# Pairing the value products of two key tiles, and multiplying query weights early, in a two-layer cross-attention kernel

## What is computed

```python
x = x + _L0_xattn_ref(_layernorm(x), ctx_2048, itok, ...)   # 16 heads, latent keys, 9 keys per query, rope
x = x + _L0_ffn_ref(_layernorm(x), ...)                     # shared expert + 8 experts, 2 chosen
x = x + _L1_xattn_ref(_layernorm(x), ctx_2048, ...)         # 16 heads of 16, all 1601 keys
x = x + _L1_ffn_ref(_layernorm(x), ...)
# in the first attention
q_c = q @ W_dq
q_nope = (q_c @ W_uq).reshape(b, lq, H, HD)
k_nope = (kv_c @ W_uk).reshape(b, lk, H, HD)
# in the second attention
attn = softmax(einsum('bnhd,bmhd->bhnm', q, k) * scale)     # over 1601 keys
o = einsum('bhnm,bmhd->bnhd', attn, v).reshape(B, N, C)
out = _qdq(o) @ _qdq(wp).T + bp
```

## Time and profile before

| | |
|---|---|
| median of 3 runs | 819.45 us (819.33 to 820.27) |
| profiled execution, its own time | 820.73 us |
| its span | 818.9 us |
| TensorE busy | 757.7 us (93%) |
| TensorE weight loads | 428.6 us (52%) |
| VectorE busy | 565.7 us (69%) |
| ScalarE busy | 383.9 us (47%) |
| GpSimd busy | 197.3 us (24%) |
| granted TensorE clock, mean | 0.979 of full speed |

### The profile page before, as it was taken

One profiled execution on the slowest core, in us unless ns is written; L12 is line 12 of the kernel. 1 busy time (PEld: TensorE's weight loads), 2 busy tenths in 40 slices (PEclk: granted clock), 3 DMA queues, 4 the chain that ended last, 5 costly groups with the idle time before them and its releaser, 6 DMA issues.

```text
span 818.9 us, 13086 instructions
## 1 busy us (share of the span) xinstructions
PE 757.7 (93%) x5026; PEld 428.6 (52%) x5027; DVE 565.7 (69%) x1290; ACT 383.9 (47%) x562; POOL 197.3 (24%) x208
## 2 busy tenths in 40 slices
PE   7999999977989989879999999999999999899996
PEld 3545767753745655644444454654455554345434
DVE  4687989531446566597787878777787777897814
ACT  2100443443423223216666657466666566574670
POOL 2298313220930131110220402300505001300000
PEclk9799999999999999999999999999999999999999
DMA  9200000205298330445055282550380820560000
GB/s 302 124 0 1 1 1 1 81 0 184 72 132 146 104 49 20 49 58 88 2 116 67 81 152 31 120 75 2 142 121 15 143 39 1 107 76 14 2 1 14
DMA packets 32476, 55.94 MB, mean 68 GB/s; under 512 B 11572, under 2 KB 20532, under 8 KB 31509
## 3 DMA queue, kind: packets, MB, share of 16 engines
q1 hardware_dynamic: 32408, 55.04, 33.5%
HBM read 42.56 MB, written 12.46 MB: 67 GB/s over the span
## 4 chain that ended last, share of the span: by engine, by line
PE 68%; DVE 18%; issue 6%; POOL 4%; ACT 2%; DMA 1%; SPq 0%; DVEq 0%; POOLq 0%; ACTq 0%
PE ps L1096 12%; PE ps L985 12%; PE ps L1075 9%; PE ps L873 5%; DVE small L1656 5%; PE ps L883 3%; PE ps L752 3%; PE ps L949 3%; PE ps L929 3%; PE ps L799 2%; PE ps L842 2%; PE ps L759 2%; PE ps L830 2%; DVE small L1606 1%; PE ps L1057 1%
## 5 line engine op out<-in xcount | busy, mean ns | idle before, releaser
L1656 DVE TENSOR_REDUCE small<-ps 128x1 f32<-128x400 f32 (+1 forms) x512 | 285.9, 572 | 83.1 <-PE ps L985 77.0
L1467 ACT ACTIVATE r<-ps 128x1024 f32<-128x1024 f32 (+1 forms) x208 | 212.6, 1024 | 90.4 <-PE ps L1075 87.7
L985 PE MATMUL ps<-r 96*128 96x400 bf16 (+1 forms) x512 | 171.3, 342 | 14.6 <-DVE small L1656 12.1
L1096 PE MATMUL ps<-r 128*17 128x256 f32 (+1 forms) x1664 | 131.2, 387 | 2.3 <-ACT r L1467 2.0
L1075 PE MATMUL ps<-r 99*128 99x256 bf16 (+1 forms) x832 | 126.5, 274 | 0.0
L985 PEld LDWEIGHTS ps<-r 96*128 96x128 bf16 x512 | 49.6, 97 | 127.3 <-DVE small L1656 93.4
L1075 PEld LDWEIGHTS ps<-r 99*128 99x128 bf16 (+1 forms) x832 | 81.6, 100 | 31.7 <-issue 9.5
L633 POOL TENSOR_TENSOR r<-r 128x400 bf16<-128x400 f32 (+1 forms) x32 | 29.4, 951 | 202.4 <-ACT r L1308 202.4
L929 PE MATMUL ps<-r,hT 128*128 128x512 f32 (+1 forms) x160 | 69.1, 564 | 0.0
L873 PE MATMUL ps<-r,wkvT 128*128 128x400 f32 (+1 forms) x128 | 53.4, 516 | 5.5 <-issue 5.5
L883 PE MATMUL ps<-wkvT,r 128*128 128x256 f32 (+1 forms) x208 | 55.5, 383 | 0.0
(11 more groups left out here) (201 smaller groups left out, 1028.4 us busy)
## 6 DMA issues: line engine op xcount, KB each, us to landing
r<-kscr SPq DMA_DIRECT2D x96, 200.1 KB, 8.8
kscr<-r SPq DMA_DIRECT2D x24, 400.2 KB, 3.8
r<-in_ctx_dram SPq DMA_DIRECT2D x4, 1601.0 KB, 7.0
r<-qscr SPq DMA_DIRECT2D x24, 128.0 KB, 5.0
r<-in_wo_dram SPq DMA_DIRECT2D x1, 2048.0 KB, 12.0
r<-in_gu_dram SPq DMA_DIRECT2D x1, 2048.0 KB, 7.7
qscr<-qpart SPq DMA_DIRECT2D x24, 64.0 KB, 1.7
x<-in_x_dram SPq DMA_DIRECT2D x1, 1024.0 KB, 5.3
```

What stands on the lines that cost most here:

```text
L985: mm(bank(ca % 2)[:, 0:m], qst[0:SROWS, h, q0:q0 + P], kst[0:SROWS, s % 2, h % HALF, a:a + m], start=True, stop=True).then_inc(mx_mm, 1)
L1096: last = mm(bank(6)[32 * k:32 * k + VW, 0:LQ], vx[0:n, b % 2, kt, h, :], pr[i % 3][0:n, k * LQ:(k + 1) * LQ], start=kt == 0, stop=kt == KT ...
L1467: fn(pr[i % 3][0:n, :], bank(2 + 2 * (i % 2), 2)[0:n, :], ACT.Exp, scale=SCALE1)\
L1656: v.tensor_reduce(mxc[quad % 2][:, n:n + 1], bank(ca % 2)[:, 0:m], AX_X, ALU.max).then_inc(mx_rdy, 1)
```

## The change

Three things. In the second layer `weigh` runs in pairs: in even steps from kt = 2 on, for the two steps before; in kt = 0 for the one before (the last of the quad before); in odd steps not at all. The chunks of maxima that `pace` puts between the two `weigh` of a pair are cut into four matmuls of 32 queries each, on the four quarters of the array's columns (`parted`). `step_work` counts the columns of the value products where they now are, so the shares of the steps in the chunks move too. In the first layer the 16 heads of L731 are issued four at a time behind the transposes of tiles 3 to 6, and the first half of L738 behind tile 5; ScalarE's copies are interleaved to match.

```diff
+def weighed(quad, kt):
+
+    i = KT * quad + kt
+    if kt == 0:
+        return [i - 1] if quad else []
+    return [i - 2, i - 1] if kt % 2 == 0 and quad < QUADS else []
+
-def step_work(jobs):
+def step_work(jobs, kt):
...
-    return 4 * LQ + 4 * LQ + sum(cost.get(kind(j), 0) for j in jobs)
+    return 4 * LQ + 4 * LQ * len(weighed(1, kt)) + sum(cost.get(kind(j), 0) for j in jobs)
@@ tensor, first layer
             for t in range(TILES):
...
                 last.then_inc(xnT_mm, 1)
-            pe.wait_ge(ld_q, 96)
-            for h in range(H):
-                last = mm(bank(h // 8)[0:QC, (h % 8) * KVC:(h % 8 + 1) * KVC], wuq[:, h, :], wuk[:, h, :],
-                          start=True, stop=True)
...
+                if t == 3:
+                    pe.wait_ge(ld_q, 96)
+                if t >= 3 and t < 7:
+                    for h in range(4 * (t - 3), 4 * (t - 3) + 4):
+                        last = mm(bank(h // 8)[0:QC, (h % 8) * KVC:(h % 8 + 1) * KVC], wuq[:, h, :], wuk[:, h, :],
+                                  start=True, stop=True)
+                        if h % 8 == 7:
+                            last.then_inc(m_mm, 1)
+                if t == 5:
+                    query_down(0)
+            query_down(1)
@@ max_scores
-                mm(bank(ca % 2)[:, 0:m], qst[0:SROWS, h, q0:q0 + P], kst[0:SROWS, s % 2, h % HALF, a:a + m],
-                   start=True, stop=True).then_inc(mx_mm, 1)
+                width = P // 4 if parted else P
+                for r in range(0, P, width):
+                    last = mm(bank(ca % 2)[r:r + width, 0:m], qst[0:SROWS, h, q0 + r:q0 + r + width],
+                              kst[0:SROWS, s % 2, h % HALF, a:a + m], start=True, stop=True)
+                last.then_inc(mx_mm, 1)
@@ the step
-                        if quad or kt:
-                            weigh(KT * quad + kt - 1)
-                        pace(4 * LQ)
+                        for i in weighed(quad, kt):
+                            weigh(i)
+                            pace(4 * LQ, parted=i < KT * quad + kt - 1)
@@ scalar, first layer
             for t in range(TILES):
...
                    ACT.Copy).then_inc(xnT_ev, 1)
+                if t == 5:
+                    act.wait_ge(ld_q, 96)
+                    weights_made(0)
+                elif t == 6:
+                    query_down(0)
+            weights_made(1)
+            query_down(1)
```

More of the change, by code:

```diff
@@ L100, in schedule @@
         window = range(max(0, first), first + KT)
-        work = [chunk_room(beside.get((i // KT, i % KT), [])) for i in window]
+        work = [chunk_room(beside.get((i // KT, i % KT), []), i % KT) for i in window]
         done, placed = 0, 0
@@ L119, in tail_bank, with chunk_room @@
     return 7 if b + 1 < B else {"turn_x": 5, "up": 0, "gate": 1, "down": 2, "expert": 3}.get(part, 7)
-def step_work(jobs):
+def weighed(quad, kt):
[4 more added lines that the diff above has]
+def step_work(jobs, kt):
     cost = {"k": 8 * 401, "v": 16 * D, "out": 2 * 4 * P, "shift": 8 * P, "up": 16 * D, "down": 16 * D,
             "expert": 16 * D, "turn_x": 4 * 4 * P, "turn_o": 4 * P, "project": 4 * D, "gate": 4 * 4 * E}
-    return 4 * LQ + 4 * LQ + sum(cost.get(kind(j), 0) for j in jobs)
-def chunk_room(jobs):
+    return 4 * LQ + 4 * LQ * len(weighed(1, kt)) + sum(cost.get(kind(j), 0) for j in jobs)
+def chunk_room(jobs, kt):
     busy = {"out": 2 * 2 * D, "bias": 2 * 2 * D, "scale": 3 * 2 * D, "round": 4 * 2 * D, "project": 2 * 2 * D,
@@ L133, in chunk_room @@
             "gate": 2 * 2 * D, "down": 3 * 2 * D, "expert": 2 * 2 * D}
-    return max(0, step_work(jobs) + 1969 - 0.6 * sum(busy.get(kind(j), 0) for j in jobs))
+    return max(0, step_work(jobs, kt) + 1969 - 0.6 * sum(busy.get(kind(j), 0) for j in jobs))
 def first_chunks(t, third):
@@ L718, in _, with query_down @@
             mm(bank(6), wkrs, kf0[1][0:KVC, :], start=True, stop=True).then_inc(rope_mm, 1)
+            def query_down(hf):
+                pe.wait_ge(xnT_ev, 4 * hf + 4)
+                for c in range(FC):
+                    last = mm(bank(4 - hf)[0:QC, :], wdq[:, c, :], xnT[:, c, hf * 512:(hf + 1) * 512], start=c == 0,
+                              stop=c == FC - 1)
+                last.then_inc(qc_mm, 1)
             for t in range(TILES):
@@ L971, in turn_q, with max_scores @@
                 last.then_inc(q1T_mm, 1)
-            def max_scores(quad, n):
+            def max_scores(quad, n, parted=False):
                 b, s, u, c = quad // 4, quad // 2, n // len(CH), n % len(CH)
@@ L1212, in _, with pace @@
                     others = [j for j in jobs if j[0] != "max"]
-                    total, count = step_work(others), len(maxima)
+                    total, count = step_work(others, kt), len(maxima)
                     passed = [0]
-                    def pace(columns):
+                    def pace(columns, parted=False):
                         passed[0] += columns
                         while maxima and (count - len(maxima)) * total < count * passed[0]:
-                            max_scores(*maxima.pop(0)[1:])
+                            max_scores(*maxima.pop(0)[1:], parted)
                     if quad < QUADS:
@@ L1248, in _, with weights_made, query_down @@
             fn(kvtok, bank(5)[:, 0:B * KVC].rearrange("p (b n) -> p b n", b=B), ACT.Copy).then_inc(kvt_ev, 1)
+            def weights_made(g):
+                act.wait_ge(m_mm, g + 1)
+                src = bank(g)[0:QC, :].rearrange("p (h n) -> p h n", h=8)
+                fn(weff[:, 8 * g:8 * g + 8:2, R:P], src[:, 0::2, :], ACT.Copy)
+                fn(weff[:, 8 * g + 1:8 * g + 8:2, 0:KVC], src[:, 1::2, :], ACT.Copy).then_inc(m_ev, 1)
+            def query_down(hf):
+                act.wait_ge(qc_mm, hf + 1)
+                fn(qcT[:, hf * 512:(hf + 1) * 512], bank(4 - hf)[0:QC, :], ACT.Copy).then_inc(qc_ev, 1)
             for t in range(TILES):
```

## The result

| | before | after |
|---|---|---|
| median of 9 runs | 820.27 us (818.32 to 822.75) | 824.25 us (820.99 to 828.18) |
| profiled execution, its own time | 820.73 us | 823.2 us |
| its span | 818.9 us | 821.4 us |

The account below looks back on a forecast made before the run. TensorE was taken to set the pace, VectorE at 76%. Second layer -16.9 + 6.3 + 11.0 = +0.4 and first layer -1.7 sum to -1.3, a median of 818.2 us; own range 815 to 822, 8 in 10 within 811 to 828.

Parts of the forecast that it names:

- The pairs, -16.9 us: Second layer: 89 pairs of value products (W) with a quartered chunk (m) between save 0.19 us each, -16.9 us.
- m is dear: Rival: second layer's quartered chunk (m) costs 0.1 to 0.5 us more, giving around 828, up to 850; chance 0.13.
- The chunks' waits, +6.3: Second layer: after 30 two-chunk odd steps the next step's first chunk waits 0.21 us for its bank, +6.3 us.
- `shift`, +11.0: Second layer, quad ends: `shift` waits for VectorE's `nst`, 0.49 us in eight quads, up to 1.24 elsewhere, +11.0 us.
- What is late next: shift: Step on second layer's quad ends: with one value product gone, `shift` must wait for `nst`, +11.0 us.
- Longer idling drops the clock: Rival, second layer: longer waits bring half clock in two to four more quads, +3.4 to +6.8, 822 to 825; chance 0.14.
- The first layer, -1.7: First layer: heads and L738's first half fill TensorE's idle time between transposes, costed at half clock, -1.7 us.
- rises a stretch earlier: First-layer case: the clock may rise earlier since L738's work now begins at 22.2, giving 29.8, 2.5 us earlier.
- my own sign: Second layer: the prediction is wrong if the steps' stretch is over 5 us shorter or longer.
- The waits are hidden: Rival, second layer: say half of the 17.3 us of waits does not appear, giving 809.5; chance 0.17.
- No change: Rival: neither layer changes, clock rising late and small costs cancelling, 819.5; no chance of its own, inside forecast's range.

Follow-up runs that it names:

- experiment 3: Changed kernel with the chunk between a pair's two value products left whole on 128 columns, not quartered; 844.9 us, 1.0295 to the kernel before.
- Experiment 6: Changed kernel with pairs of value products in odd steps 3 to 11 and single ones in steps 0, 1 and 12; 816.88 us, 0.9957 to the kernel before.
- experiment 2: Kernel before with only the second layer's parts of the change, first layer untouched; 827.78 us, 1.0084 to the kernel before.
- experiment 1: Kernel before with only the first layer's part of the change, second layer untouched; 816.52 us, 0.9955 to the kernel before.
- experiment 4: Changed kernel with a quad's chunks of maxima ending one step earlier, in kt = 9 instead of 10; 821.54 us, 1.0009 to the kernel before.
- 5 even shares: Kernel of experiment 4 with the constant in `chunk_room` cut from 1969 to 400; 819.57 us, 0.9994 to the kernel before.
- experiment 7: Kernel of Experiment 6 with the constant in `chunk_room` cut from 1969 to 400; 811.52 us, 0.9894 to the kernel before.

## Why the prediction was wrong

**The pairs, -16.9 us: right, and under-sized.** 0.22 us a pair in the timelines of the changed kernel and of experiment 3, against the 0.19 I counted. The sums have -22.8 us for the steps, with the pairs of quad 15, which I had at 0.06 us each and left out; they gain nothing. "m is dear" is refuted by 0.17 us from start to start; its four narrow weight loads take 0.12 us together (553.69, above), beside the W in front, and do not show in the time. The estimate by the Trainium skill (TensorE: Matmul & The Clock Gate, LDWEIGHTS) was 107 ns for the four one behind the other. The trace does not bear it out: one load of a whole chunk has a record of 0.10 us and the four narrow ones 0.12 together, so they overlap.

**The chunks' waits, +6.3: the mechanism right, the sum too high.** The 0.2 us waits are in the trace where I put them. But chunks wait only 2.0 us more in all. 2.9 us of the difference are the two waits that now stand in front of `shift` (above). The rest may be that VectorE catches up while TensorE stands before `shift`, which I named and took nothing off for; no run isolates it.

**`shift`, +11.0: +14.0**, or 11.1 without the 2.9 us that were chunk waits before. In five undisturbed quads it is 0.57 us (forecast 0.49), in quads 4 and 8 1.14 (1.24), in quads 0 and 14 0.88 and 0.86 (0.86 each), in the three late ones 2.1 to 2.2 (2.4, 1.9 and 1.9). What I did not see is quads 5, 9 and 13, 1.4 each in place of 0.62. The timeline of the first of them:

```profile
527.87 0.17 DVE L1691 TENSOR_TENSOR nst<-small,nst 128x8 bf16<-128x8 f32 x1
527.96 0.88 DVE L1845 SCALAR_TENSOR_TENSOR y<-ps,small,mag 128x256 f32<-128x256 f32 x2
...
528.89 0.61 PE L1073 MATMUL ps<-identb,nst 128*3 128x128 bf16 x8 [1.31 <-DVE y L1845]
```

`nst` is ready at 528.04, but `shift` writes bank 7, and that is free only when VectorE has made `y` from it, 0.8 us later. I had traced the data of `shift` and not its bank. In time it mattered little: behind the same operation TensorE stood 0.3, 0.3 and 1.3 us in these quads before.

**The step that failed: "What is late next: shift".** I stopped there, and the terms for K, V, the tail and the clock stood at nothing. The W's in odd steps had covered a second kind of wait, that of K, V and the tail for bank 7 and ScalarE's copies out of it; I noted for those steps only that they have matmuls enough "and do not wait". The timeline of one:

```profile
571.66 0.59 ACT L1332 ACTIVATE r<-ps,bk 128x400 bf16<-128x400 f32 x1
...
572.30 0.94 PE L886 MATMUL ps<-r,wkvT 128*128 128x400 f32 x2 [0.39 <-ACT r L1332]
```

By the sums K waits 3.8 us, V 1.9 and the tail 5.2, where before the three had 1.9 together: **+9.0 us that no term of mine held**. No experiment isolates them. Experiment 6, which moves the pairs to the odd steps but keeps bare steps, leaves them nearly as they are (4.2, 0.6, 5.0) and is faster than the changed kernel even so, which speaks for a price of pairing rather than of the place of the pairs, but does not show it. W itself waits 0.8 less.

**The clock.** I had "Longer idling drops the clock" as a rival with 0.14, at 822 to 825, and the median lies there. That is partly luck: the rival counted with the other terms as I had them, and their errors cancel (+6.9 and +1.9 against -5.9 and -2.4, below). The profile has 13.7 us at half clock in the steps for 6.8, at the late `shift`s where the forecast looked: one drop is new (584.60), one is where it was, and one is longer (704.07 to 710.90, 6.83 us). That is +3.4, the low end of the rival's price, in one more quad and not in two to four. The profile of experiment 2 has the same three. Over all executions the change is smaller: the mean granted clock falls from 0.9785 to 0.9765 by the second layer's parts alone, and from 0.983 (experiment 1) to 0.979 with them on top, worth 1.3 and 2.5 us by the slope in the last section.

That long waits bring the drop is not shown. The wait of 1.64 us was followed by one before and is followed by none in experiment 1's profile, and experiment 6 has waits of 1.97, 2.07 and 2.51 us in the same quads and full clock through all its steps. With the clock's +3.4 but without the missed +9.0, and with the pairs at their real price, the second layer would have come out slightly ahead.

**The first layer, -1.7: -4.5 (experiment 1).** The path was right: transposes, heads, passes, query matmuls. The rate was wrong. I ran the heads and passes at half clock because the trace of before had them so the earlier trace rows, and my case of a clock that "rises a stretch earlier" was the best one I allowed. That clock belonged to the idle time that the edit fills, in six of the seven profiles with it. Of the 7.1 us by which the query matmuls come earlier 4.1 arrive at the steps. VectorE's operations, matched in order, are 7.1 us earlier at 43 us, 6.1 at 94 to 175 and 5.2 from 223 to 320; the changed kernel then has half clock from 362.7 to 366.2 us, where the kernel before has none. What takes the rest away no run isolates.

**The sum**, in the measured terms: second layer -22.8 + 14.0 + 2.0 + 9.0 - 0.8 + 3.4 + 1.9 unassigned = +6.7, first layer -4.1, together +2.6, as the spans have it (+2.5); the medians, +4.0, lie a little above. The steps came out 6.3 us worse than forecast (+6.7 for +0.4): all waits together cost 6.9 more than the 17.3 I had, the clock 3.4 and the unassigned 1.9, and the pairs gave 5.9 back. The first layer gave another 2.4. By my own sign, the steps over 5 us longer (6.9), the prediction was wrong. "The waits are hidden" fell by both `shift` and K. "No change" is outside the interval.

## What to carry to other kernels

Two matmul groups of the same column layout belong together, and what must stand between them can take that layout: 0.22 us for each pair that is formed, at no cost for a 400-column bf16 matmul in four quarters. But a group that is moved was also cover, and for each step that it leaves one must ask for every later matmul both when its data is ready and when its output bank is read out, on VectorE and on ScalarE. Put the cover back in front of the longest chain (experiment 6) before tuning shares. The even shares took 5.4 us off experiment 6 by the medians, of which the clock accounts for 2.4 (last section), and 2.0 us off experiment 4, inside the noise; only with both did pairing pay. When an edit fills idle time of TensorE, cost its work at both levels of the clock, and not at the one that the old trace shows there.

## What the runs showed of the hardware that I had not expected

**Why the small operations are slow in three quads.** The timeline of the changed kernel at the first of these, with GpSimd's rows:

```profile
462.46 0.50 DVE L1687 TENSOR_SCALAR nst<-small 128x8 bf16<-128x8 f32 x1
...
462.99 0.17 DVE L1688 SCALAR_TENSOR_TENSOR small<-small,nst 128x8 f32<-128x8 f32 x1
463.00 2.76 POOL L651 TENSOR_TENSOR r<-r 128x401 bf16<-128x401 f32 x3
463.20 0.81 DVE L1690 CAST nst<-small 128x8 bf16<-128x8 f32 x1
464.04 0.86 DVE L1691 TENSOR_TENSOR nst<-small,nst 128x8 bf16<-128x8 f32 x1
...
465.04 0.75 PE L1073 MATMUL ps<-identb,nst 128*3 128x128 bf16 x6 [2.14 <-DVE nst L1691]
```

The three GpSimd operations take 0.92 us each (2.76 / 3), so they end at 463.92, 464.84 and 465.76. VectorE's cast ends at 464.01 and its last operation at 464.90: both, which take 0.18 us elsewhere, end just behind one of GpSimd's. In the steps of this profile 60 operations of eight columns write or read `nst`: the 51 that start while GpSimd is idle take at most 0.18 us, and the nine that start inside one of its operations 0.44 to 0.86. In experiment 4 it is the same (GpSimd's ends at 579.34, 580.26, 581.17 by the same division, VectorE's at 580.29 and 581.20). The Trainium skill says that VectorE, in an operation with two inputs in SBUF or in a two-port mode, and GpSimd take a shared pair of ports for a whole instruction, and that the other is blocked meanwhile (SBUF — State Buffer, SBUF: two separate sides). The operations with two inputs agree with it; whether the cast, with one, runs in such a mode no run shows. The reductions out of PSUM beside GpSimd keep their 0.57 us. No run moved GpSimd's work away, so that this alone would end the 2 us waits is not shown.

**A clock that an edit keeps up.** Of the seven profiles of kernels with the first layer's part, six have full clock from 16.98 us through the passes. The seventh, experiment 3, whose first layer is the same, has half from there to 23.81, and its next stretch at full. So that part of the gain does not come in every execution; the medians hold it in whatever share it came.

**What an execution's clock is worth.** Within each kernel the executions differ in their mean granted clock, and the time follows it: fitted over the executions of all nine kernels, each about its own kernel's mean, it is 0.63 us less for each 0.001 more, and 0.57 to 0.67 in each kernel by itself but those of experiments 2 and 3 (0.85 and 0.32, from six and four executions). By this fit (an estimate) the kernels' mean times at one clock, 0.980, are:

```
                        mean us   mean clock   at clock 0.980
before, first set         821.1        0.979            820.1
before, second set        820.9        0.979            820.2
changed                   824.7        0.979            824.3
1 first layer alone       816.9        0.983            819.0
2 second layer alone      827.4        0.977            825.2
3 whole chunk             845.1        0.976            842.6
4 window earlier          821.6        0.981            822.5
5 even shares             820.2        0.982            821.2
6 odd pairs               816.7        0.984            819.2
7 odd pairs, shares       811.6        0.988            816.5
```

So about 3 of the 4.2 us of experiment 1 are clock, and more than half of what experiment 7 gains over the kernel before (5.5 of 9.3). At one clock experiment 7 is 3.7 us ahead of the kernel before, and experiments 1 and 6 about 1 us.
